# Out projection of the first attention, look-up network and norms by token halves, on one Trainium2 core

## The reference

```python
# layer 0, attention: q, k, v, z per head; convolution, rotary, gates over 4 lags give out
rms = jax.lax.rsqrt(jnp.mean(out * out, axis=-1, keepdims=True) + EPS_NORM)   # over all 16 heads
out = out * rms * norm_w * _silu(z)
x = x + ga * (out @ Wout)                       # 2048 -> 256
h = _layernorm(x) * (1 + cb) + sb               # norm "n1"
x = x + gb * _L0_ffn_ref(h, lut, gate_idx, up_idx, down_idx)  # silu(h@G) * (h@U) @ Dn, weights lut[idx]
# layer 1
h = _layernorm(x) * (1 + ca) + sa               # norm "n2"
x = x + ga * _L1_attn_ref(h, ...)               # softmax attention, 16 heads, weights code * scale
```

## Time and profile before

| | us |
|---|---|
| median of 3 runs | 1172.76 |
| lowest, highest | 1170.27, 1174.37 |
| the profiled execution | 1174.85 |
| its span (first to last instruction) | 1173.0 |
| PE busy | 1035.0 (88%) |
| DVE busy | 752.6 (64%) |
| ACT busy | 552.7 (47%) |
| POOL busy | 285.8 (24%) |

### The profile page before, as it was taken

The page is one execution under the profiler, slowest core; times in us unless marked ns, Lnnn a source line. Parts: engine busy times, 40 slices in busy tenths (PEclk is TensorE's granted clock), DMA queues, the critical chain, the costliest instruction groups (busy, mean ns, idle before and its releaser), DMA issues.

```text
span 1173.0 us, 16828 instructions
## 1 busy us (share of the span) xinstructions
PE 1035.0 (88%) x5771; PEld 818.5 (70%) x5771; DVE 752.6 (64%) x1275; ACT 552.7 (47%) x1081; POOL 285.8 (24%) x243
## 2 busy tenths in 40 slices
PE   6779999999999959747976999999997997669987
PEld 5568988989889834323435998998996454458876
DVE  1378998998989839953126778778777135423344
ACT  1056878788788658900113565556554022113320
POOL 0004234243342400021002212211210004336660
PEclk8589999999999979978997999999998999689996
DMA  7038778778676860080001011101100101158944
GB/s 262 1 82 160 167 154 172 160 163 188 149 157 161 198 140 1 0 197 1 0 0 55 28 54 54 47 33 54 54 0 0 68 1 66 55 187 276 273 144 185
DMA packets 77374, 121.59 MB, mean 104 GB/s; under 512 B 25028, under 2 KB 54415, under 8 KB 76561
## 3 DMA queue, kind: packets, MB, share of 16 engines
q1 hardware_dynamic: 65296, 86.91, 24.8%
q0 software_dynamic: 12032, 34.11, 15.2%
HBM read 70.31 MB, written 38.08 MB: 92 GB/s over the span
## 4 chain that ended last, share of the span: by engine, by line
PE 72%; DVE 15%; issue 4%; ACT 3%; DMA 3%; POOL 2%; DVEq 0%; POOLq 0%; SPq 0%; ACTq 0%
PE psum L604 8%; PE psum L606 8%; PE psum L605 8%; PE psum L838 5%; PE psum L964 5%; PE psum L656 5%; PE psum L924 4%; PE psum L627 4%; PE psum L811 3%; PE psum L704 3%; PE psum L719 2%; PE psum L974 2%; DVE arena L1410 2%; PE psum L757 2%; DVE arena L1313 2%
## 5 line engine op out<-in xcount | busy, mean ns | idle before, releaser
L1313 DVE SCALAR_TENSOR_TENSOR arena<-arena,par_in 128x1024 f32<-128x1024 f32 x144 | 183.5, 1284 | 35.7 <-ACT arena L1041 26.1
L604 PE MATMUL psum<-lut_w_r,arena_r 128*128 128x512 f32 x320 | 132.1, 413 | 17.0 <-POOL arena_r L1741 10.1
L605 PE MATMUL psum<-lut_w_r,arena_r 128*128 128x512 f32 x320 | 127.9, 400 | 0.0
L606 PE MATMUL psum<-lut_w_r,arena_r 128*128 128x512 f32 x320 | 127.6, 399 | 0.0
L1725 POOL DMA_DIRECT2D arena<-arena x64 | 53.8, 983 | 214.4 <-DVE arena L1325 214.2
L1142 ACT ACTIVATE arena<-psum,small 128x256 f32<-128x256 f32 x128 | 59.3, 473 | 86.0 <-DVE small L1452 86.0
L604 PEld LDWEIGHTS psum<-lut_w_r,arena_r 128*128 128x128 f32 x320 | 61.4, 192 | 30.2 <-issue 10.1
L1031 ACT ACTIVATE arena<-psum 128x1024 f32<-128x1024 f32 x48 | 49.3, 1026 | 66.3 <-PE psum L606 65.8
L604 PE MATMUL psum<-arena_r 128*128 128x256 f32 x256 | 77.8, 304 | 1.5 <-DVE arena_r L1477 1.5
L1772 POOL DMA_INDIRECT out_rows<-arena x64 | 62.7, 980 | 46.9 <-DVE arena L1626 24.7
L1741 POOL TENSOR_TENSOR arena_r<-arena,arena_r 128x512 fp32r<-128x512 f32 x16 | 21.2, 1325 | 216.3 <-ACT arena_r L1153 216.3
...
...
## 6 DMA issues: line engine op xcount, KB each, us to landing
...
```

The costliest lines, as they stand in the source:

```text
L604: nc.tensor.matmul(dst, w_l, x_h, start=start, stop=False, skip_group_check=True)
L605: nc.tensor.matmul(dst, w_h, x_l, start=False, stop=False, skip_group_check=True)
L606: return nc.tensor.matmul(dst, w_h, x_h, start=False, stop=stop, skip_group_check=True)
L1313: nc.vector.scalar_tensor_tensor(by_batch(dst), by_batch(u[s])[:, :, j:j + S], par_in[:, bass.ds(M_CW + (w * H + h) * TAPS + j, 1)], by_ba ...
```

## The change

- The weights of the look-up network move from a tensor of their own (`lut_w`) to the end of `G`. `w_out` goes to another place in the arena and is loaded in two halves, from the start of turn 16's idle time on, among the loads of the indices; its waits for the rotary DMAs go. The first load of the second attention's weights waits for head 15 in `G` only.
- PE starts the first token half of the out projection in turn 16, before the scores of head 15, and sets further parts of it between that head's steps. From there on everything goes by halves of 512 tokens: the norm of the first half (`n1a`) stands among the second half's projection, that of the second half (`n1b`) among the first half's gate and up matmuls, `n2a` among the second half's, and `n2b` among head 0's q, k and v of the first half.
- The down matmuls of a half no longer alternate with the gate and up matmuls; they come after all six blocks, and the products of six blocks are kept.
- Look-up chunks 0 and 1 move into turn 16, chunk 2 into turn 17, and the rest stand between the steps of the root mean square, the residuals, the norms and the first products. The bits 1 to 3 go to SBUF (`lut_bits`) in place of PSUM.
- On POOL the four half norms' 1/sqrt stand among the weights of head 0, the 128x4096 product and the weights of head 1. That product's loads wait for `attn_out` 4, the whole projection, as before.
- The number of matmuls of the projection and of the network stays: 64, 48 and 24 of 512 columns. A half norm's variance takes 8 matmuls with tokens on the partitions, and its result needs no transpose.

```diff
@@ -111,7 +118,8 @@
 
         x_t, h_t = sb("x_t", KC * T), sb("h_t", KC * T)
         cst, par_in = sb("cst", C_ALL), sb("par_in", M_ALL)
-        lut_w, lut_w_r = twice("lut_w", LUTC)
+        G, halves = twice("G", H * T + LUTC)
+        lut_w, lut_w_r = G[:, H * T:H * T + LUTC], halves[:, H * T:H * T + LUTC]
...
         lut_v, lut_b0 = [lv0, lv1], [lb0.bitcast(I32), lb1.bitcast(I32)]
...
+        lut_bits = gm0[:, 0:3 * LC]
...
-        (wo_s,) = carve(H * D, base=9 * T)
+        wo_s = G[:, 12 * T:12 * T + H * D]
...
+        def part_stat_dve(dve, tag, n):
+            dve.wait_ge(*norm(tag, "var"))
+            nc.vector.tensor_scalar(stat[:, n * HN:(n + 1) * HN], bank(5)[:, 0:HN], 1.0, 1e-5, ALU.mult, ALU.add)\
+                .then_inc(norm(tag, "stat")[0], 1)
+
+        def part_rstd_pool(pool, tag, n):
+            pool.wait_ge(*norm(tag, "stat"))
+            nc.gpsimd.tensor_tensor(rstd[:, n * HN:(n + 1) * HN], stat[:, n * HN:(n + 1) * HN], neg_half[:, 0:HN], ALU.pow)\
+                .then_inc(norm(tag, "rstd")[0], 1)
+
+        def part_diag_dve(dve, tag, n, d):
+            dve.wait_ge(*norm(tag, "rstd"))
+            nc.vector.tensor_tensor(by_tile(d[:, 0:512]), over_tiles(ident, HN), over_cols(rstd[:, n * HN:(n + 1) * HN], P), ALU.mult)\
+                .then_inc(norm(tag, "diag")[0], 1)
...
             sp.dma_start(lut_idx[:, LPRE:LUTC - LPOST].rearrange("p (h c) -> p h c", c=LW),
-                         a["idx"].rearrange("h p c -> p h c")).then_inc(sg("in_idx"), 16)
-            sp.dma_start(lut_idx[:, LUTC - LPOST:LUTC], a["idx_post"]).then_inc(sg("in_idx"), 16)
-            for s in "qk":
-                sp.wait_ge(sg("a0_rope_" + s), 32 * H)
-            sp.dma_start(wout, a["w_out"]).then_inc(sg("in_wout"), 16)
+                         a["idx"].rearrange("h p c -> p h c")).then_inc(again("in_idx_b")[0], 16)
+            sp.dma_start(wout[:, H * D // 2:H * D], a["w_out"][:, H * D // 2:H * D]).then_inc(again("in_wout_b")[0], 16)
+            sp.dma_start(lut_idx[:, LUTC - LPOST:LUTC], a["idx_post"]).then_inc(again("in_idx_c")[0], 16)
             sp.wait_ge(sg("a0_sq_rows"), 16 * H)
-            sp.dma_start(ln_sq[:, 0:T], sq_rows).then_inc(sg("in_sq"), 16)
-
-            sp.wait_ge(sg("lut_done"), LCH)
-            sp.wait_ge(sg("attn_out"), KC)
+            sp.dma_start(sq_in, sq_rows).then_inc(sg("in_sq"), 16)
 
             def load1(h):
                 sp.dma_start(code, a["qkv_codes"][h]).then_inc(sg("a1_code"), 16)
@@ -526,7 +590,9 @@
                     sp.dma_start(scl[32 * g:32 * g + 32, :], a["qkv_scales"][h][g:g + 1, :].broadcast_to([32, QKV]))\
                         .then_inc(sg("a1_code"), 16)
 
+            sp.wait_ge(sg("a0_gT"), H)
             load1(0)
+            sp.wait_ge(sg("attn_out"), 2 * KC)
             sp.dma_start(wo_c, a["wo_codes"]).then_inc(sg("in_wo"), 16)
             for g in range(4):
                 sp.dma_start(wo_s[32 * g:32 * g + 32, :], a["wo_scales"][g:g + 1, :].broadcast_to([32, H * D]))\
...
+                    i = nc.tensor.matmul(out_bank(n, m), wout[:, h * D + m * P:h * D + m * P + P],
+                                         G[:, h * T + n * 512:h * T + n * 512 + 512], start=(h == 0), stop=(h == H - 1))
+                return i
 
             def turn(h, hh, par, st, zq):
...
                     t.then_inc(sg("a0_vT"), 1)
+                    if is_last(h):
+                        pe.wait_ge(*again("in_wout_a"))
+                        pe.wait_ge(sg("a0_ssq_s"), H)
+                        pe.wait_ge(sg("a0_gT_sb"), H - 2)
+                        project_out(0, 0, range(0, 7))
 
                     pe.wait_ge(sg("a0_rope_q"), 32 * h)
...
+                        pe.wait_ge(*again("in_wout_b"))
+                        project_out(0, 0, range(7, 10))
                 if 1 in st:
                     pe.wait_ge(sg("a0_sq_q"), h + 1)
...
+                    if is_last(h):
+                        pe.wait_ge(sg("a0_gT_sb"), H - 1)
+                        project_out(0, 0, range(10, 14))
 
...
+            project_out(0, 0, range(14, 15))
+            pe.wait_ge(sg("a0_v_tok"), H)
+            project_out(0, 1, range(0, 14))
             pe.wait_ge(sg("a0_gT_sb"), H)
+            spread_pe(pe, "r0", fb)
+            project_out(0, 1, range(14, 15))
+            for m in range(KC):
+                project_out(0, m, range(15, 16)).then_inc(sg("attn_out"), 1)
             pe.wait_ge(sg("a0_on"), H)
+            project_out(1, 0, range(0, 5))
+            half_mean_pe(pe, "n1a", 0, 0)
+            project_out(1, 0, range(5, 13))
+            part_var_pe(pe, "n1a", fsq)
+            project_out(1, 0, range(13, 16)).then_inc(sg("attn_out"), 1)
+            project_out(1, 1, range(0, 4))
+            part_spread_pe(pe, "n1a", fb)
+            project_out(1, 1, range(4, 16)).then_inc(sg("attn_out"), 1)
+
...
+            pe.wait_ge(*norm("n1a", "out"))
+            pe.wait_ge(sg("lut_done"), -(-2 * UPC // LC))
+            gate_up(0, 0)
+            gate_up(0, 1)
+            half_mean_pe(pe, "n1b", 1, 1)
+            gate_up(0, 2)
+            gate_up(0, 3)
+            part_var_pe(pe, "n1b", fsq)
+            gate_up(0, 4)
+            gate_up(0, 5)
+            part_spread_pe(pe, "n1b", fb)
             pe.wait_ge(sg("lut_done"), LCH)
+            down(0)
+            pe.wait_ge(*norm("n1b", "out"))
+            gate_up(1, 0)
+            gate_up(1, 1)
+            half_mean_pe(pe, "n2a", 0, 2)
+            gate_up(1, 2)
+            gate_up(1, 3)
+            part_var_pe(pe, "n2a", gsq)
+            gate_up(1, 4)
+            gate_up(1, 5)
+            part_spread_pe(pe, "n2a", gb)
+            down(1)
+
...
             pe.wait_ge(sg("in_lo"), 2 * KC)
+            pe.wait_ge(sg("a1_w_lo"), 1)
+            project_by_halves(slot(0), 0, 0, (0,))
+            half_mean_pe(pe, "n2b", 1, 3)
+            project_by_halves(slot(1), 0, 1, (0,))
+            part_var_pe(pe, "n2b", gsq)
+            v_tiles(slot(3), 0, range(0, HN))
+            part_spread_pe(pe, "n2b", gb)
+            pe.wait_ge(sg("in_lo"), 3 * KC)
+            project_by_halves(slot(0), 0, 0, (1,)).then_inc(sg("a1_q"), 1)
+            project_by_halves(slot(1), 0, 1, (1,)).then_inc(sg("a1_k"), 1)
+            v_tiles(slot(3), 0, range(HN, NT)).then_inc(sg("a1_v"), 1)
...
+            lut_dve(2)
+            dve.wait_ge(sg("in_sq"), 16)
+            nc.vector.tensor_reduce(stat, by_tile(sq_in), AX.X, ALU.add).then_inc(sg("rms_sum"), 1)
+            dve.wait_ge(sg("rms_sum"), 1)
+            nc.vector.tensor_scalar(stat, stat, 1.0 / (H * HD), 1e-6, ALU.mult, ALU.add).then_inc(norm("r0", "stat")[0], 1)
+            lut_dve(3)
+            dve.wait_ge(*norm("r0", "rstd"))
+            nc.vector.tensor_tensor(by_tile(fb), over_tiles(ident, NT), over_cols(rstd, P), ALU.mult).then_inc(norm("r0", "diag")[0], 1)
+            lut_dve(4)
+            attn_half(0)
+            lut_dve(5)
+            part_centre_dve(dve, "n1a", 0, fc)
+            lut_dve(6)
+            part_stat_dve(dve, "n1a", 0)
+            lut_dve(7)
+            part_diag_dve(dve, "n1a", 0, fb)
+            lut_dve(8)
+            part_modulate_dve(dve, "n1a", 0, 0, fc, SB_, CB)
+            lut_dve(9)
+            lut_dve(10)
+            attn_half(1)
+            product_f(0, 0)
+            lut_dve(11)
+            product_f(0, 1)
+            part_centre_dve(dve, "n1b", 1, fc)
+            lut_dve(12)
+            product_f(0, 2)
+            product_f(0, 3)
+            part_stat_dve(dve, "n1b", 1)
+            product_f(0, 4)
+            part_diag_dve(dve, "n1b", 1, fb)
+            product_f(0, 5)
+            part_modulate_dve(dve, "n1b", 1, 0, fc, SB_, CB)
+            ffn_half(0)
+            product_f(1, 0)
+            product_f(1, 1)
+            part_centre_dve(dve, "n2a", 0, gc)
+            product_f(1, 2)
+            product_f(1, 3)
+            part_stat_dve(dve, "n2a", 0)
+            product_f(1, 4)
+            part_diag_dve(dve, "n2a", 0, gb)
+            product_f(1, 5)
+            part_modulate_dve(dve, "n2a", 0, 1, gc, SA, CA)
+            lower_in(0)
+            ffn_half(1)
+            part_centre_dve(dve, "n2b", 1, gc)
+            part_stat_dve(dve, "n2b", 1)
+            part_diag_dve(dve, "n2b", 1, gb)
+            part_modulate_dve(dve, "n2b", 1, 1, gc, SA, CA)
+            lower_in(1)
...
@@ -1728,7 +1932,7 @@
             for h in range(H + 2):
                 turn(h, h // 2, h % 2, ((1,) if h < H else ()) + ((2,) if 0 < h <= H else ()) + ((3,) if h > 1 else ()))
             rstd_pool(pool, "r0")
-            rstd_pool(pool, "n1")
+            part_rstd_pool(pool, "n1a", 0)
 
             def weights(h, par):
                 pool.wait_ge(sg("a1_code"), 80 * (h + 1))
@@ -1742,10 +1946,12 @@
                     .then_inc(sg("a1_w_lo"), 1)
 
             weights(0, 0)
+            part_rstd_pool(pool, "n1b", 1)
             pool.wait_ge(sg("in_wo"), 80)
```

(3 more changed lines are left out.)

418 lines of the change are left out of this document (239 added, 179 removed).

## The result

| | before, us | changed, us |
|---|---|---|
| median of 4 runs | 1171.64 | 1119.47 |
| lowest, highest | 1170.27, 1174.37 | 1115.17, 1120.57 |
| profiled execution | 1174.85 | 1119.4 |
| its span | 1173.0 | 1117.6 |

The ratio is 0.956, with a 95% interval from 0.9528 to 0.9591: faster, by 52.2 us between the medians. The forecast was 1126. Of the 6.5 us between it and the measured median about 5 lie in the stage and 1.1 in the median of before, which a fourth run moved from 1172.76 to 1171.64.

A forecast was written before the change was run, and what follows sets the result against it. PE bounds the kernel, so time is won where it waits. Work 151.3 plus waits and clock 27.0 gives a stage of 178.3 us instead of 224.8, 46.5 less: forecast 1126, own range 1119 to 1133, with rivals 1112 to 1142.

The forecast's parts named there:

- Step 1: Tail of head 15: PE waits 5.6 us before the scores, as w_out's load pushes the rotary DMA; bounds 0.5 to 8.3.
- Step 2: Root mean square in the projection: PE waits 2.4 and 0.3 us, 2.7 together, for sum of squares and gate; bounds 0 and 6.
- Step 3: Norm n1a among the projection's second half: its ACT and DVE steps are covered by matmuls and cost PE nothing.
- Step 4: Look-up chunks of 4.4 us ahead of the second half's residual and n1b's squares: PE waits 1.5 and 1.2, together 2.7 us.
- rival of 5.8 us per chunk: Look-ups bind on DVE and ACT: ten chunks add 10 us and the two waits 4, time 1140; chance 0.20.
- Step 5: n1b's spread: POOL's 128x4096 product shuts out DVE's diagonal for its whole length, PE waits 5.0 us; bounds 0 and 7.7.
- rival of a late load: Product's loads come after 510.5 or POOL is held up, so it misses n1b's diagonal: 5 us less, 1121; chance 0.17.
- Step 6: Norm n2b and head 0, with little work to put beside the chain: PE waits 9.0 us; bounds 7.4 and 12.
- Step 7: Low granted clock after PE's remaining short pauses in the stage: 2 us, bounds 0 and 8.
- rival of a lower clock throughout: PE without pauses is granted less clock; gain gone under a stage mean of 0.76, 1189 us at 0.70; chance 0.02.
- signs of being wrong: PE waiting on ACT or DVE in the projection's second half, chunks over 5 us, or projection clock under 0.9.
- first rival: Product does not meet n1b's diagonal, since loads come after 510.5 or POOL is held up: 1121 us; chance 0.17.

The follow-up runs named there:

- mul_after_out: The changed kernel, with POOL's 128x4096 product waiting until n1b's result is written: median 1123.76 us, ratio 0.9556 to the kernel before.
- mul_in_8: The changed kernel, with POOL's 128x4096 product issued as eight pieces of 512 columns in the same place: 1124.76 us, ratio 0.9542 to the kernel before.

## Why the prediction was right, and where it missed

Steps are counted as in the prediction. The stage was put at 178.3 us and is 173.3; the work of 151.3 leaves 22.0 us for waits and clock where 27.0 were expected. Of the 22.0 us, 14.5 are idle time of PE and 7.5 are busy time beyond the work at full clock.

- **Step 1, rotary DMA, 5.6 us: measured 0.** This is the step that failed, and it is as large as the whole miss of 5.0; the other steps miss by 1.5 or less and nearly cancel. The bounds, 0.5 to 8.3, missed it too. The scores start 5.85 us behind the transposes, right behind the seven heads, and before at 6.46. What failed is the push of 5 us by `w_out`. The step took the earlier trace rows's 0.97 for full engines and let `w_out` travel "ahead of and beside" the DMA from then on; its second half has landed 2.3 us before the stage begins. The first rotary DMAs are pushed (7.49 us to landing for 3.52 before), the last one is not (8.39 for 9.29): it lands 5.5 us into the stage, 6.4 before. Seven heads cover that by 0.4 us only. Why the last one escapes stays open. The 128 GB/s stood in the same row as the share.
- **Step 2, sum of squares, 2.7: measured 2.2** at the spread, by the mechanism told (sum, chunk 3 and diagonal one after the other on DVE). The squares came back 1.95 us after DVE was ready for them. All of it comes some 6 us earlier in the stage than told, mostly because step 1's wait is not there.
- **Step 3, cover of n1a, 0: measured 0.9** at its spread. Head 0's weights on POOL (460.81, 2.12 us) held a group of three selections of DVE for 3.01 us instead of 1.38, and the diagonal came 1.6 late. The cover of "a chunk in front of each step" was right but for this.
- **Step 4, look-ups, 2.7: measured 1.6.** The chunk's pitch is 4.36 us (4.4 expected), since three bits to SBUF take 0.81 and not 1.32. The second part, n1b's squares, came to 0. The rival of 5.8 us per chunk falls.
- **Step 5, the large product, 5.0: measured 3.7** of wait, and 1.7 of low clock behind it. Place, cause and releaser are as told: product at once behind n1b's 1/sqrt, diagonal 6.56 us, PE waiting for L368. All of it lies some 5 us earlier in the stage than expected. The rival of a late load falls: the last scales landed at 497.02, 1.1 us before POOL was free for the product. That it was so close is luck in part; a load later by 4 us would have let the diagonal go first. mul_after_out and mul_in_8 confirm the cause: take the product away or cut it, and the wait goes.
- **Step 6, n2b and head 0, 9.0: measured 8.6** (22.2 us from the last down matmul less 13.6 of work): 5.9 us of waits, and 2.7 of busy time beyond the work, mostly low clock, which the step had not named. The block by head 1's weights is there, 1.6 us. The 1/sqrt of a half takes 1.01 us, not the full norm's 1.64.
- **Step 7, clock, 2: measured 3.5** outside head 0: 1.8 behind the root mean square's wait and 1.7 behind the product's. The rival of a lower clock throughout falls: the dense windows are at 0.94 to 1.00.

0 + 2.2 + 0.9 + 1.6 + 3.7 + 8.6 + 3.5 = 20.5 of the 22.0; 1.5 us are not traced to a place. The waits among these terms make 14.3 us of the 14.5 idle, so what is left is busy time.

Of the signs that the prediction named, three held: the wait at n1b's spread with a diagonal of over 6 us, 22 us from the last down matmul to the end of v, and chunks at 4.4. The wait of 5 us before the scores did not come. "No wait of PE over 2 us" before the spread of n1b was broken by the 2.19 at the root mean square, and contradicted the 2.4 of its own step 2. The wait of 0.86 us on DVE in the projection's second half is one of the signs of being wrong, if a small one.

The measured 1119.47 lies at the low end of the forecast's own range, nearer to the 1121 of the first rival (the product does not meet the diagonal) than to 1126. By the number alone that rival would look right; the trace shows the product meeting the diagonal in full. Faster had a chance of 0.97. Steps 1, 5 and 6 and the worth of n1a's place were tested by experiments; steps 2 and 4 are read from the trace alone, and step 3's block likewise.
